# Local attention on one Trainium2 core: who copies the output out of PSUM, who normalises it, and when the gelu table is loaded

## The reference, cut to what matters

```
sim  = einsum('bhwid,bhwjd->bhwij', q * 8, k)       # 8 heads of 64, windows of 64 and the one before
attn = softmax(where(mask, -max, sim))
out  = einsum('bhwij,bhwjd->bhwid', attn, v)
x = x + out @ wo
h = layernorm(shift_token(x)) * lg + lb
a, g = split(h @ w1 + b1);  x = x + (a * gelu(g)) @ w2 + b2
```

## Time and profile before

| what | value |
| --- | --- |
| median of 3 runs | 665.0 us (664.74 to 666.1) |
| profiled execution, span from first to last instruction | 674.0 us; the page gives no time of its own beside this |
| mean granted clock of TensorE over the span | 0.973 |
| PE, DVE, ACT, POOL busy | 585.9, 516.2, 368.2, 300.5 us |
| chain that ended last | PE 50%, DVE 25%, issue 12%, ACT 7%, POOL 3% |
| ACT table loads | 39, mean 1.283 us |
| POOL's power of `ssq` (L659) | 32, mean 2.962 us |
| fill of the slot table from the zeros, on SP's queue | 1 DMA, 1548 KB, 7.6 us to landing |

### The profile page before, as it was taken

One profiled execution on the slowest core, in us unless ns is written; L12 is line 12 of the kernel. 1 busy time (PEld: TensorE's weight loads), 2 busy tenths in 40 slices (PEclk: granted clock), 3 DMA queues, 4 the chain that ended last, 5 costly groups with the idle time before them and its releaser, 6 DMA issues.

```text
span 674.0 us, 14407 instructions
## 1 busy us (share of the span) xinstructions
PE 585.9 (87%) x5382; PEld 341.8 (51%) x5382; DVE 516.2 (77%) x919; ACT 368.2 (55%) x586; POOL 300.5 (45%) x254
## 2 busy tenths in 40 slices
PE   3577887999999999999999888878999999878994
PEld 2235655656767657667566556433232334444441
DVE  6787988889788888887898745897777757566772
ACT  0235353567576675765665573414756577436772
POOL 3465464554545554555656433413200010442776
PEclk9979999999999999999999899987999999999998
DMA  8303010010101010101110034344792343115441
GB/s 273 77 16 120 17 34 9 18 33 10 33 17 26 18 25 18 27 15 24 27 26 18 17 94 110 77 71 93 200 232 103 130 156 109 68 36 115 59 53 9
DMA packets 33297, 44.03 MB, mean 65 GB/s; under 512 B 9248, under 2 KB 24652, under 8 KB 32460
## 3 DMA queue, kind: packets, MB, share of 16 engines
q1 hardware_dynamic: 29260, 40.99, 23.0%
q0 software_dynamic: 3968, 2.12, 2.5%
HBM read 27.54 MB, written 8.41 MB: 53 GB/s over the span
## 4 chain that ended last, share of the span: by engine, by line
PE 50%; DVE 25%; issue 12%; ACT 7%; POOL 3%; DMA 2%; POOLq 0%; another core or an unknown queue 0%; DVEq 0%; SPq 0%; ACTq 0%
PE ps L1601 5%; PE ps L1632 4%; PE ps L1823 3%; PE ps L1610 3%; DVE smx L1089 3%; PE ps L1737 3%; DVE ssum L1059 3%; DVE mneg L1291 2%; ACT region_r L895 2%; PE ps L1487 2%; PE ps L1554 2%; PE ps L1502 2%; PE ps L1721 2%; PE ps L1488 2%; PE ps L1573 2%
## 5 line engine op out<-in xcount | busy, mean ns | idle before, releaser
L659 POOL TENSOR_TENSOR rnorm<-ssum_c,neg_half 128x16 f32<-128x16 f32 x32 | 94.8, 2962 | 102.5 <-DVE ssum_c L1062 101.1
L667 POOL TENSOR_TENSOR region_r<-region_b,region_w 128x512 f32<-128x512 f32 x60 | 77.8, 1316 | 43.9 <-DVE region_b L1067 43.4
L1291 DVE TENSOR_REDUCE mneg<-ps 128x2 f32<-128x1024 f32 x64 | 77.2, 1220 | 18.7 <-PE ps L1721 17.6
L895 ACT ACTIVATE region_r<-ps 128x1024 f32<-128x1024 f32 x64 | 63.2, 1024 | 34.2 <-PE ps L1737 34.1
L788 ACT ACTIVATE region_w<-ps 128x1024 f32<-128x1024 f32 x32 | 32.8, 1026 | 53.3 <-PE ps L1488 51.9
L764 ACT ACT_TABLE_LOAD x39 | 50.0, 1283 | 1.4 <-PEq L1970 0.7
L1487 PE MATMUL ps<-region_w,hT 128*128 128x512 f32 x64 | 36.9, 660 | 15.1 <-DVE region_b L1067 14.2
L624 POOL TENSOR_TENSOR var_eps<-mv,eps 128x4 f32<-128x4 f32 x20 | 4.5, 223 | 100.6 <-DVE mv L1004 100.6
L751 POOL DMA_INDIRECT out<-region_r x24 | 37.7, 1571 | 24.4 <-DMA out<-xr 11.3
L1601 PE MATMUL ps<-region_w 128*114 128x512 f32 x96 | 47.2, 615 | 0.6 <-ACT region_w L805 0.6
L1067 DVE TENSOR_TENSOR region_b<-ps,rnorm 128x1024 f32<-128x1024 f32 x32 | 39.1, 1223 | 8.1 <-POOL rnorm L659 7.1
(11 more groups left out here) (287 smaller groups left out, 1413.5 us busy)
## 6 DMA issues: line engine op xcount, KB each, us to landing
region_w<-in_wx SPq DMA_DIRECT2D x16, 768.0 KB, 4.4
region_b<-region_w SPq DMA_DIRECT2D x56, 130.0 KB, 2.3
parts_dram<-region_b SPq DMA_DIRECT2D x6, 384.0 KB, 2.6
xs_dram<-region_w SPq DMA_DIRECT2D x1, 1548.0 KB, 7.6
region_w<-in_wqkv SPq DMA_DIRECT2D x2, 768.0 KB, 8.4
pts<-xs_dram SPq DMA_DIRECT2D x24, 64.0 KB
region_w<-parts_dram SPq DMA_DIRECT2D x3, 384.0 KB, 6.9
region_b<-parts_dram SPq DMA_DIRECT2D x3, 384.0 KB, 7.4
```

Source lines behind the costliest of these rows:

```text
L659: g.tensor_tensor(rnorm[:, :], ssum_c[n % 2][:, :], neg_half[:, :], ALU.pow).then_inc(S["rnormed"], 1)
L667: g.tensor_tensor(dst, src, tab, ALU.mult).then_inc(S["rot_bb"], 1)
L895: act_(dst, bank(l1_bank[what, b, i], of=2), ACT.Exp).then_inc(T["ex"], 1)
L1291: d.tensor_reduce(mneg[b % 2][:, 2 * i:2 * i + 2], bank(l1_bank[what, b, i], of=2) .rearrange("p (q t) -> p q t", q=2), AX.X, ALU.max, neg ...
```

## The change

`o_out` on DVE, which read the output from PSUM, is split in three. ScalarE copies the raw output with its column of sums from banks 4 and 5 to a new SBUF buffer `o_raw` at step `vals` (`outputs_raw`), and this copy now releases the banks. DVE takes the reciprocal of the sums from `o_raw` at a new step `onorm`, which stands behind `rotsum` and `ff_rstd` (`o_weights`). POOL multiplies at the same step and writes `o_sb` (`weighted`). The gelu table load moves from ahead of `v` to behind `masks`. To make room, the gelu buffer now lies in the zeros with which a DMA fills the experts' slot table, and the first gelu waits for that DMA.

```diff
--- before.py
+++ after.py
@@ -98,9 +98,10 @@
         v_al = [part(region_a, NT * HEADS * VW).rearrange("p (t h d) -> p t h d", t=NT, h=HEADS) for _ in range(2)]
         qT = [part(region_a, HP * SEQ).rearrange("p (h t) -> p h t", h=HP) for _ in range(2)]
         sq = part(region_a, 2 * INNER)
-        gel = part(region_a, SEQ)[0:HW]
         ZEROS = 4 * ROW
         zeros = part(region_a, ZEROS)
+        gel = zeros[0:HW, 0:SEQ]
+        o_raw = part(region_a, 2 * 4 * VW).rearrange("p (b h d) -> p b h d", b=2, h=4)
         used["region_a"] = EXP * 2 * INTER - SEQ - 4 * P
         wq, wk, wvg, bvg = (part(region_a, P) for _ in range(4))
         hnT = part(region_a, SEQ)
@@ -255,7 +256,7 @@
             "ln_stats", "ln_mv", "ln_eps", "ln_rstd", "ln_out", "ln_neg", "ln_act", "xnT_mm", "scanned", "bc_mm", "x1",
             "yT_mm", "hT_lo", "hT_hi", "qk_mm", "v_mm", "squared", "ssq", "ssq_c", "rnormed", "normed", "rot_a",
             "rot_bb", "rotated", "v_sb", "qkT_mm", "qT_sb", "kT_sb", "s_mm", "smax", "diffed", "pT_mm", "exped", "o_mm",
-            "o_rec", "o_norm", "oT_mm", "oT_sb", "wo_mm", "y_att", "hs_lo", "hs_mm", "hs_hi", "based_y", "based",
+            "o_raw", "o_rec", "o_norm", "oT_mm", "oT_sb", "wo_mm", "y_att", "hs_lo", "hs_mm", "hs_hi", "based_y", "based",
             "hnT_mm", "hnT_sb", "up_mm", "gelued", "acted", "down_mm", "y_out", "stored")}
         x_in = [sem(f"x_in{b}") for b in range(BATCH)]
         v_off_in = [sem(f"v_off_in{t}") for t in range(NT)]
@@ -349,7 +350,6 @@
                 t, k = i % NT, i // NT - 1
                 up = {3: HC * k, 0: HC * (k - 1) + 1, 1: HC * (k - 1) + 2, 2: -1}[t]
                 yield from of(NTILES, ("probs", i))
-                yield from of(BLOCKS * HC, ("to_gelu", up))
                 yield from of(NTILES, ("v", i + 3), ("ssq", i + 3))
                 yield from early.get(i, ())
                 if t == 0:
@@ -360,6 +360,7 @@
                 if t == 1:
                     yield from of(BLOCKS, ("ff_stats", k))
                 yield from of(NTILES, ("vals", i), ("heads", i + 1), ("masks", i + 1))
+                yield from of(BLOCKS * HC, ("to_gelu", up))
                 yield from behind_heads.get(i, ())
                 if t == 0:
                     yield from of(BLOCKS, ("shift", k))
@@ -372,7 +373,7 @@
                 yield from of(NTILES, ("rotsum", i + 2))
                 if t == 1:
                     yield from of(BLOCKS, ("ff_rstd", k))
-                yield from of(NTILES, ("norm", i + 3))
+                yield from of(NTILES, ("onorm", i), ("norm", i + 3))
                 yield from of(BLOCKS * HC, ("up", up))
                 if t == 2:
                     yield from of(BLOCKS, ("down", k - 1))
@@ -658,6 +659,13 @@
                 need(pool, S["normed"], n)
                 g.tensor_tensor(rnorm[:, :], ssum_c[n % 2][:, :], neg_half[:, :], ALU.pow).then_inc(S["rnormed"], 1)
 
+            def weighted(n):
+                pool.wait_ge(S["o_rec"], n + 1)
+                need(pool, S["oT_mm"], n - 1)
+                g.tensor_tensor(o_sb[n % 2].rearrange("p (b h d) -> p b h d", b=2, h=4), o_raw[:, :, :, 0:DH],
+                                orec[n % 2][:, :, :].unsqueeze(3).to_broadcast([P, 2, 4, DH]), ALU.mult)\
+                 .then_inc(S["o_norm"], 1)
+
             def rotate(n):
 
                 pool.wait_ge(S["normed"], n + 1)
@@ -735,6 +743,8 @@
                     power(ln_no["ff_stats", n])
                 if what == "ssq":
                     inverse_lengths(n)
+                if what == "onorm":
+                    weighted(n)
                 if what == "rot" and n >= DVE_TURNS:
                     rotate(n)
                 if what == "base":
@@ -814,6 +824,12 @@
                     act_(pts[n % 2][:, z * HP:(z + 1) * HP, :].rearrange("p h q -> p (h q)"), bank(6 + z), ACT.Exp)\
                         .then_inc(S["exped"], 1)
 
+            def outputs_raw(n):
+                a.wait_ge(S["o_mm"], n + 1)
+                need(a, S["o_norm"], n)
+                act_(o_raw.rearrange("p b h d -> p b (h d)"),
+                     bank(4, of=2).rearrange("p (b n) -> p b n", b=2)[:, :, 0:4 * VW], ACT.Copy).then_inc(S["o_raw"], 1)
+
             def outputs_sb(n):
                 a.wait_ge(S["oT_mm"], n + 1)
                 need(a, S["wo_mm"], n - 1)
@@ -836,6 +852,8 @@
                 l, c = m // (HC * BATCH), m % HC
                 a.wait_ge(S["up_mm"], m + 1)
                 need(a, S["acted"], m)
+                if m == 0:
+                    a.wait_ge(M["zeroed"], 16)
                 act_(gel, ps[0:HW, (up_bank(m) + 1) * BANK:(up_bank(m) + 2) * BANK], ACT.Gelu, bias=b1[:, l, 1, c:c + 1]).then_inc(S["gelued"], 1)
 
             def silu(n):
@@ -934,6 +952,8 @@
                     heads_sb(n)
                 if what == "probs":
                     exponentials(n)
+                if what == "vals":
+                    outputs_raw(n)
                 if what == "oT":
                     outputs_sb(n)
                 if what == "shift":
@@ -1092,16 +1112,10 @@
                 d.tensor_tensor(sdiff[n % 2], sc, smx[n % 2][:, :].unsqueeze(2).to_broadcast([P, HEADS, P]),
                                 ALU.subtract).then_inc(S["diffed"], 1)
 
-            def o_out(n):
-                ob = bank(4, of=2).rearrange("p (b n) -> p b n", b=2)[:, :, 0:4 * VW]\
-                    .rearrange("p b (h d) -> p b h d", h=4)
-                v.wait_ge(S["o_mm"], n + 1)
-                d.reciprocal(orec[n % 2][:, :, :], ob[:, :, :, DH]).then_inc(S["o_rec"], 1)
-                v.wait_ge(S["o_rec"], n + 1)
-                need(v, S["oT_mm"], n - 1)
-                d.tensor_tensor(o_sb[n % 2].rearrange("p (b h d) -> p b h d", b=2, h=4), ob[:, :, :, 0:DH],
-                                orec[n % 2][:, :, :].unsqueeze(3).to_broadcast([P, 2, 4, DH]), ALU.mult)\
-                 .then_inc(S["o_norm"], 1)
+            def o_weights(n):
+                v.wait_ge(S["o_raw"], n + 1)
+                need(v, S["o_norm"], n - 1)
+                d.reciprocal(orec[n % 2][:, :, :], o_raw[:, :, :, DH]).then_inc(S["o_rec"], 1)
 
             def y_att(k):
                 ys = y[k % BATCH]
@@ -1384,8 +1398,8 @@
                     rotate(n)
                 if what == "scores":
                     scores_out(n)
-                if what == "vals":
-                    o_out(n)
+                if what == "onorm":
+                    o_weights(n)
                 if what == "y_att":
                     y_att(n)
                 if what == "ff_stats":
@@ -1544,7 +1558,7 @@
                 p = k % 2
                 pe.wait_ge(v_off_in[t], 16 * (2 if t else 1) * (k + 1))
                 pe.wait_ge(S["v_sb"], n + 1)
-                claim((4, 5), (S["o_norm"], n + 1))
+                claim((4, 5), (S["o_raw"], n + 1))
                 for j in range(HEADS):
                     if j % HP == 0:
                         pe.wait_ge(S["exped"], 2 * n + j // HP + 1)
```

## The result

The changed kernel takes 673.5 us (median of 4 runs, 672.7 to 674.3), the kernel before 664.87 in the same comparison: ratio 1.0131, interval 1.0091 to 1.0170, so 8.6 us slower (6.0 to 11.3). The forecast was 671.9.

What follows compares the result with a forecast made beforehand. It saw no plain bound overall (PE busy 87%, DVE 77%), with PE busy 44.57 of 45.8 us in blocks. Terms -3.3 (blocks, tile 6) + 4.5 (front) + 4.8 (tail) + 0.9 = +6.9 gave 671.9 us; own range 668 to 676, 8-in-10 664 to 679.

Steps and rivals of the forecast that it cites:

- Blocks: Five four-tile blocks from tile 7 on: each gains 1.7 - 0.6 - 0.5 = 0.6 us, together -3.0 us.
- first tile: First tile of a block: transposes wait for POOL's product behind `rotsum` and the reciprocal; 0.5 us given back.
- not slower: Rival: lighter DVE removes all PE's waits for it, 2.6 us a block; 661.9 us in all; chance 0.15.
- third tile: Third tile of a block: PE waits for POOL's product behind its powers until about 253.75; 0.6 us given back.
- mask term: Blocks: the mask matmuls' wait for DVE goes, at most 1.7 us a block.
- Front: Tiles 0 to 5: product ahead of `project_qk` costs 2.6 us, late raw copy 2.2, tile 4 regains 0.3; +4.5 us.
- Clock: Loss of PE's clock in tile 29, none in the front; +0.9 us in the total.
- Tail: Tiles 27 to 31: +3.9 us in tile 29, +0.6 in 27, +0.5 in 31, -0.2 in 30; +4.8 us.
- Tile 29: Tail: product queues behind POOL's split pieces and `ff_rstd`, delayed by the table load; `project_o` at 401.9, not 398.01: +3.9 us.
- Load at nothing: Blocks: later gelu table load fits in ScalarE's 4.1 us idle before its gelus; costed at nothing.
- No effect: Rival: front and tail waits lie beside others and the block gain pays the rest; about 665.5 us; chance 0.08.
- Dearer: Rival: DVE and POOL disturb each other where PE waits for the product, some 8 tiles; +7.5, 679.4 us; chance 0.17.

Runs made afterwards that it cites:

- e9: Both parts of the change in tiles 0 to 6 only, all other tiles as in the kernel before; 1.0147 times the kernel before.
- e10: Both parts of the change in tiles 27 to 31 only, all other tiles as in the kernel before; 1.0153 times the kernel before.
- e11: Changed kernel plus 20 filling transposes on PE ahead of the wait for the product, in tiles 1 and 4 only; 1.0170 times the kernel before.
- e4: Changed kernel plus 20 filling transposes on PE ahead of the wait for the product, in tiles 0 to 5; 1.0230 times the kernel before.
- e7: Changed kernel with tile 29's two layer-1 split pieces moved behind the product; 670.3 us, 1.0105 times the kernel before.
- e12: Changed kernel with the gelu table load back at its old early place, raw copy path in all tiles; 1.0187 times the kernel before.
- e2: Kernel before with only the gelu table load moved late, DVE still normalising from PSUM in all tiles; 1.0039 times the kernel before.
- e8: Both parts of the change in tiles 7 to 26 only, the rest as in the kernel before; 662.8 us, 0.9972 times the kernel before.
- e1: Raw copy path in tiles 7 to 26 only, late table load in all, otherwise the kernel before; 1.0003 times the kernel before.

## Why the forecast was right, and where it was not

**Blocks: -3.0 forecast for the five blocks, -3.7 measured** (tile 6 is counted in the front here). The mask wait is gone in all four tiles. But the 1.7 us that I put down for it is what the weight loads waited. The matmuls themselves waited less in that block of the first trace, and once more for DVE, ahead of the second tile's transposes:

```profile
PE ps L1514 <- DVE region_r L1102: 0.8, 3, 0.4
...
PE ps L1539 <- DVE region_b L1092: 0.2, 1, 0.2
```

Counted from the start of each tile the masks start 0.08, 0.24, 0.47 and 0.29 us earlier in the changed kernel, 1.1 in all. The first tile gives back 0.45 to the product, as forecast (0.5), and is 0.25 shorter even so, because two waits of PE for DVE are gone too, 0.25 ahead of `project_qk` and 0.2 ahead of the next tile's transposes; that much of the rival "not slower" is there. PE in a first tile of the changed kernel, answering to the earlier trace rows:

```profile
189.10 0.41 PE L1528 MATMUL ps<-mask_b,ident_b 64*64 64x512 bf16 x4
...
193.38 0.66 PE L1576 MATMUL ps<-ident,region_r 128*128 128x128 f32 x4 [0.45 <-POOL region_r L665]
```

In the third tile I had 0.6 given back to the product. The product took 1.04 and not 1.27 and was just in time. The tile gains nothing all the same (10.79 us in both kernels): behind the mask wait lay a second one. The feed-forward matmuls `up_l0` need the bank that the first head copy empties, and this copy waits for PE's head transposes, not for the raw copy. PE and ScalarE there, answering to the earlier trace rows:

```profile
255.70 1.09 PE L1516 MATMUL ps<-ident,region_r 128*128 128x128 f32 x8
256.72 0.41 PE L1528 MATMUL ps<-mask_b,ident_b 64*64 64x512 bf16 x4
257.57 1.94 PE L1615 MATMUL ps<-region_w 128*114 128x512 f32 x4 [0.44 <-ACT region_w L815]
```

```profile
256.83 0.60 ACT L815 ACTIVATE region_w<-ps 128x512 f32<-128x512 f32 x1 [0.41 <-PE ps L1516]
```

From the head transposes to `up_l0` it is 1.87 us here and was 1.88 before (249.15 to 251.03); only the name of the wait has changed. So a block gains 0.25 + 0.24 + 0 + 0.19 = 0.7 us. The forecast's 0.6 came from 1.7 - 0.6 - 0.5. In the traces the masks give 1.1, the third tile loses its 0.5 again and the first 0.45, and 0.4 to 0.5 come from waits for DVE that the forecast left as they were. The mask term was 0.6 too large and the other gain was missing; that they nearly cancelled is luck.

**Front, tiles 0 to 6: +4.2 forecast (+4.5, and -0.3 in tile 6), +8.2 measured.** The six traces on the old path average 84.99 us, the five on the new 93.20. PE's busy time over the same instructions went from 70.15 to 73.24 on average. So the waits made 5.1 us, close to my 4.2, and the clock 3.1. Here the forecast failed: the step "Clock" put one loss of 0.9 us in tile 29 and none in the front, where the earlier trace rows had already shown half speed after an idle of under 1 us, and where I had just forecast four longer ones. A new wait must be priced with what runs behind it.

**Tail: +4.8 and a clock loss of 0.9 forecast, +4.8 measured** up to tile 31 (48.48 us over before's two traces and e9, 53.31 over the changed kernel's two, e10 and e11; e4's 56.80 is not in it), and 0.4 more inside tile 31. Tile 29 went as worked out, its clock loss too: it grew from 11.25 to 16.05 us, by 4.8 where 3.9 + 0.9 was forecast. The small terms were off: tile 27 lost 0.3 and not 0.6, tile 30 lost 0.4 and did not gain 0.2. Tile 29 began 3.54 us later than in before's first trace; less that, the product ended at 400.25 where the forecast said 400.6, and `project_o` began at 402.11 (401.9). e7 shows the cause, the split pieces ahead of the product, and e12 that the late load, ahead of those pieces, makes 1.5 of the 4.05 us.

**Load at nothing:** right in blocks (e2). In the tail 1.4 us of it was counted inside tile 29, close to the 1.5 of e12; e2 shows that it costs 1.9 with the old path too.

**Sum.** +8.2 - 3.7 + 4.8 = 9.3 us, within the measured 6.0 to 11.3. The forecast's 6.9 had the product's price and the mask wait too high and the front's clock missing. The sign and the main places were worked out; how near the total came is in part luck, since the front was forecast at half of what it cost, and the stages do not make up the whole time: behind the attention the second trace of the changed kernel is 3.6 us shorter than that of before (252.34 against 255.92), which no term had. Of the signs that the prediction gave, the masks' wait in tiles 0, 3 and 5 only, the blocks' length (45.1 us) and the wait of over 4 us near 400 us came; the wait in each third tile did not.

**The rivals.** Not slower: the blocks would have had to reach 43.8 us; they are 45.1, since PE is busy for 44.2 of them. No effect: e9 and e10 refute it. Dearer: its mechanism is there, at other places than the new product, which took 1.04 us in all 32 tiles. Once a block GpSimd's power now starts beside DVE's `rotsum`, which reads two operands from SBUF; in the changed kernel, POOL and DVE:

```profile
176.81 3.81 POOL L660 TENSOR_TENSOR rnorm<-ssum_c,neg_half 128x16 f32<-128x16 f32 x1 [4.21 <-DVE ssum_c L1082]
```

```profile
176.64 1.22 DVE L1104 TENSOR_TENSOR region_r<-region_r 128x1024 f32<-128x1024 f32 x1
```

The power takes 2.90 us otherwise, so it lost 0.91, where the DVE instruction had 1.05 left to run. By this rule the trace agrees: the Trainium skill, "SBUF — State Buffer", section "SBUF: two separate sides", has the two exclude each other for a whole instruction. The pair at 44.31, which the prediction set against one DVE product, lay beside two with two SBUF operands each, `rotsum` at 44.15 and `scale_cos` at 45.28: each product of the pair lost about 0.9 to one of them, and `scale_cos` took 2.28 us itself. So it goes the other way too: in the changed kernel once a block DVE's `scale_cos` took 1.67 us and not 1.22 while GpSimd's pair of `rotate` ran. Neither shows as a wait of PE, since in the blocks PE never waits for `normalise` any more.

**Open.** (1) Why e9 and e10 are slower by their ratios (9.8 and 10.2 us) than their stages (9.2 and 5.9). Part lies in the routed experts, where PE waits for gathered rows. The kernel before, second trace:

```profile
614.93 0.33 PE L1812 MATMUL ps<-ident,pts 128*128 128x128 f32 x1 [2.77 <-DMA pts<-xs_dram]
...
616.34 1.07 PE L1823 MATMUL ps<-region_b,region_r 128*32 128x512 f32 x3
```

The changed kernel, second trace:

```profile
622.76 0.33 PE L1850 MATMUL ps<-ident,pts 128*128 128x128 f32 x1 [0.72 <-DMA pts<-xs_dram]
...
623.71 0.60 PE L1861 MATMUL ps<-region_b,region_r 128*32 128x512 f32 x3
```

2 us more of wait and half the clock behind it: 3.4 us in all, and the execution of before that shows them was 3.7 above its median. The longest such wait was 2.1 to 2.6 us in the traces of e7, e8, e9, e10 and e12 as well, 1.5 in e11, and under 1 in the changed kernel's two, in the first trace of before and in those of e1 to e4. Whether it depends on the attention's end or falls by chance, one trace of each can't tell. Span against span of before's second trace, e10 is 7.0 us longer (673.0) and e9 10.3 (676.3). (2) 0.8 of e2's 2.7 us. (3) Why the front's clock differs between executions of the same instructions. (4) Where half of e8's gain goes, and how the front's cost divides between the copy and the later place.

## What to carry to other kernels

Take work off an engine only where another engine waits for that very work, stage by stage: the same edit gained 3.7 us where PE was the bound and lost 13 at the two ends. When an instruction moves to an in-order engine, add up what stands ahead of it in its queue, in the busiest step and not in the mean one; the 4 us of tile 29 came out of a before-trace to 0.4. When a wait goes, look for the one that ends next: in the third tile of a block it came 0.4 us later and took back the whole gain. And read a wait from the matmuls, not from the weight loads beside them (0.8 against 1.7 us a block). Last, price each new wait of TensorE twice, once as idle time and once as the clock of what follows.
